# Twelve layers on one core: norms in halves, weight loads moved into the layers, one reordered load queue and one merged last layer

## Chip, cores and metric

The kernel runs on one core of one Trainium2 chip. The metric is the device time of one execution in microseconds (us), given as the median of several runs. All arithmetic is in float32.

## The reference, cut to what matters

A stream x of 8 batches x 64 tokens x 256 features goes through four blocks of three layers, each of the form x + f(layernorm(x)): L0_xattn, L0_attn, L0_ffn, L1_xattn and so on to L3_ffn.

```python
def _layernorm(x, axis=-1, eps=1e-05):
    m = jnp.mean(x, axis=axis, keepdims=True)
    v = jnp.var(x, axis=axis, keepdims=True)
    return (x - m) / jnp.sqrt(v + eps)
...
    x = x + _L0_xattn_ref(ctx_1024, _layernorm(x, axis=-1), mask_BxS2_bf1, ...)
    x = x + _L0_attn_ref(_layernorm(x, axis=-1), ...)
...
    x = x + _L2_xattn_ref(_layernorm(x, axis=-1), ctx_1024, ctx_1024, mask_BxSxS2_ff0, L2_xattn_Wq, L2_xattn_Wk, L2_xattn_Wv)
...
    x = x + _L3_ffn_ref(_layernorm(x, axis=-1), L3_ffn_W_qkv, L3_ffn_b_qkv, L3_ffn_W_gate, L3_ffn_b_gate, L3_ffn_W_experts, L3_ffn_b_experts)
```

The four xattn layers read a context of 8 x 1601 rows of 256 numbers. L0_xattn is a perceiver attention with 16 heads, whose keys are the normed context and the latents. L1_xattn is attention of 16 heads with one mask for all batches. L2_xattn is one head over the context, with a mask of its own for each batch (softmax of q times context plus mask, times context). L3_xattn is linear attention. The attn layers are self attention (L0, L3) and mamba scans (L1 both ways, L2). The ffn layers are mixtures of experts, and the last one, L3_ffn, is self attention and a mixture side by side, both of the same normed input:

```python
        attn = jnp.einsum('bqhd,bkhd->bhqk', q, k) / jnp.sqrt(jnp.asarray(hd, x.dtype))
        attn = jax.nn.softmax(attn, axis=-1)
        attn_out = jnp.einsum('bhqk,bkhd->bqhd', attn, v).reshape(B, S, D)
        gate = jax.nn.softmax(x @ W_gate + b_gate, axis=-1)
        top_g, top_i = jax.lax.top_k(gate, TOP_K)
        combine = jnp.sum(jax.nn.one_hot(top_i, E, dtype=x.dtype) * top_g[..., None], axis=2)
        expert_out = jnp.einsum('bsd,edf->bsef', x, W_experts) + b_experts
        moe_out = jnp.einsum('bsef,bse->bsf', expert_out, combine)
        return attn_out + moe_out
```

## The kernel before, in words

`program` (L3930) lays out one block of instructions per layer after another. Inside a block each engine has its own hand-written program and the engines meet at semaphores only; at the end of a block all engines meet, and `end_layer` (L519) clears the layer's semaphores. x lies as `x_tok`, NT = 4 tiles of P = 128 tokens x 256 features. Two buffers, `weights_a` and `weights_b`, hold a layer's weights and the next layer's: before each layer but the last, a block of its own (L3950 to L3953) has SP issue the load of the next layer's weights (`load_weights`, L3941).

Nearly every layer begins alike. VectorE (DVE) in `norm_vector` (L173) takes bn_stats of the four tiles (L178), bn_aggr (L181), adds epsilon (L183); ScalarE (ACT) in `norm_scalar` (L192) makes the reciprocal root by Ln and Exp (L196, L198); DVE then writes the normed `z_tok` tile by tile (L187) and signals once. TensorE (PE) meanwhile multiplies the identity with constants (`keep_busy`, L201, matmul at L204, 512 columns each, two calls, or four for the mamba), then `turn_tensor` (L207, L218) turns the eight 128x128 squares of z into PSUM; `zT` (in the trace `z_feat`) is copied from there, feature half 0 by ACT and half 1 by DVE, and the first projection waits for both.

**L0_xattn** (L770). Ahead of the main loop DVE norms the latents twice and scales them (L974, L975), norms the first batch's context tile group by group (`ctx_stats` L950, `ctx_norm` L965, scaled by GpSimd (POOL) at L1126 and L1128), and only then takes part in the loop over eight query pairs p (PE L1262 and L1270, ACT, DVE L1005). ACT has `ctx_rstd` (L1156) ahead of its loop as well.

**L1_xattn** (L1452). SP loads the first batch's context (L1545), the mask (L1549), and the other seven; two buffers. The next layer's weights were issued ahead of these, by the block before.

**L2_xattn** (L540). Four pairs u of batches. For each batch the context is loaded twice, with features on partitions (`ctx_feat`, L602, a ring of 3 buffers) and with tokens on partitions (`ctx_tok`, L532 and L533, a ring of 3), and for each pair two mask halves (`mask`, L607). SP issues in one order and stands at each wait: a feature buffer is free when the scores of its batch are done, a token buffer when its `mix` is done. PE runs `scores(0)`, and then for each u `scores(u+1)`, `turn_weights(u)`, `mix(u)` and `turn_mixed(u)`:

```python
                        if b >= RING:
                            sp.wait_ge(scored, (b - RING) // 2 + 1)
                        sp.dma_start(cT[b % RING][:, :, :], L.aps["ctx_feat"][b].rearrange("(k p) n -> p k n", p=P)
...
                        if b >= RING:
                            sp.wait_ge(mixed, (b - RING) // 2 + 1)
                        load_ctx_tok(sp, ck[b % RING], L.aps["ctx_tok"][b], ck_loaded[b % RING])
```

**L3_ffn** (L3807) calls `self_attention` (L222), a block, and then `experts` (L2623), another. The attention goes over four tiles: PE projects V (L440), q and k (L447), makes scores (L457), turns the weights (L465), weighs V (L476) and turns the result back (L486); DVE copies scores (L325), subtracts the maximum (L329, L330), divides (L336 to L338) and adds to x (L345, L352); `keep_busy` fills waits of PE at four places. `experts` begins with the gate (PE L2843, DVE L2588 to L2620, PE L2861), then has for each of 8 experts PE's eight matmuls (L2899) into one PSUM tensor and DVE's four scaled additions into x (L2772), one after the other, and ends with a bias matmul (L2911) and an addition (L2787).

## Time and profile before

| | |
|---|---|
| median of 3 runs | 3185.78 us (3185.38 to 3188.05) |
| profiled execution | 3181.54 us, its span 3179.8 us |
| mean granted TensorE clock | 0.947 of full speed |
| PE busy | 2795.1 us (88%) |
| DVE, ACT, POOL busy | 1643.3, 1091.3, 522.6 us (52%, 34%, 16%) |
| DMA | 271.40 MB, mean 85 GB/s |

The layers begin at these times of the profiled execution (us from the span's start), read off SP's first issue or the first norm instruction of each:

| | xattn | attn | ffn |
|---|---|---|---|
| L0 | 8 | 1253 | 1308 |
| L1 | 1353 | 1857 | 2152 |
| L2 | 2375 | 2512 | 2608 |
| L3 | 2774 | 3008 | 3062 |

In the profile L12 is line 12 of the kernel; PE is the matmul part of TensorE, PEld its weight loads, SPq the queue of SyncE's DMA issues. A bracket behind an instruction says how long its engine stood idle before it and what released it. "PEclk" is the granted clock as a share of full speed. Layer prefixes are left out of names: `L_ffn_expert_w` belongs to whichever ffn layer is running at that time.

### The profile page before, as it was taken

The numbers are of one execution on the slowest core, as the hardware profiler recorded it, in microseconds if no ns is written. First come the engines' busy times: TensorE is split into PE (matmuls) and PEld (weight loads), VectorE is DVE, ScalarE is ACT, GpSimd is POOL, SyncE is SP. The second block draws the span as 40 slices with busy tenths as digits, with TensorE's granted clock in tenths as the row PEclk, the third lists the DMA queues.
The fourth block names the chain that finished last, engine by engine and source line by source line (L and its number), as shares of the span: only waits on it lengthen the run. The fifth ranks groups of instructions, "written<-read, shape, count | busy, mean of one in ns | idle before, by whom it ended". The sixth has DMA issues, their size and how long they took to land. (4 is left out here: it accounts for less than half of the span.)

```text
span 3179.8 us, 43613 instructions
## 1 busy us (share of the span) xinstructions
PE 2795.1 (88%) x17456; PEld 1893.7 (60%) x17456; DVE 1643.3 (52%) x3618; ACT 1091.3 (34%) x1933; POOL 522.6 (16%) x280
## 2 busy tenths in 40 slices
PE   5899999999999998779999978998975689799876
PEld 2466666666666666545656535665962357688644
DVE  5556465655656443545555545763541250177563
ACT  2333333333333332225555436641321252211120
POOL 2112020202112000000000004761010041144200
PEclk8899999999999999889999989998987799899898
DMA  4123223131323211130100000115857338543001
GB/s 141 46 54 67 64 59 78 44 78 45 67 55 67 55 45 34 69 125 22 43 22 22 1 6 34 43 32 187 304 193 250 107 88 301 207 166 124 33 1 33
DMA packets 92096, 271.40 MB, mean 85 GB/s; under 512 B 7920, under 2 KB 57096, under 8 KB 85240
## 3 DMA queue, kind: packets, MB, share of 16 engines
q1 hardware_dynamic: 87896, 259.65, 26.9%
q0 software_dynamic: 2976, 8.13, 0.7%
q8 instruction: 138, 2.26, 0.3%
q10 hardware_dynamic: 1024, 0.86, 0.1%
q14 instruction: 62, 0.51, 0.1%
HBM read 256.64 MB, written 11.44 MB: 84 GB/s over the span
## 5 line engine op out<-in xcount | busy, mean ns | idle before, releaser
L1375 PE MATMUL L_xattn_bank<-L_xattn_keys_tok,L_xattn_probsT 119*128 119x257 f32 (+1 forms) x1792 | 451.5, 392 | 9.2 <-ACT L_xattn_probsT L1211 0.4
L1312 PE MATMUL L_xattn_wide<-L_xattn_keys_feat,weights_a 128*128 128x512 f32 (+2 forms) x1024 | 382.9, 517 | 1.3 <-DVE L_xattn_k_rnorm L1024 0.7
L1375 PEld LDWEIGHTS L_xattn_bank<-L_xattn_keys_tok,L_xattn_probsT 119*128 119x128 f32 (+1 forms) x1792 | 320.0, 190 | 96.1 <-issue 33.1
L1312 PEld LDWEIGHTS L_xattn_wide<-L_xattn_keys_feat,weights_a 128*128 128x128 f32 x1024 | 190.4, 191 | 151.8 <-issue 125.4
L1020 DVE COPY L_xattn_k_normed<-L_xattn_wide 128x833 f32<-128x833 f32 (+1 forms) x128 | 131.3, 1026 | 227.6 <-PE L_xattn_wide L1312 227.6
L2313 DVE TENSOR_TENSOR_SCAN L_attn_state<-L_attn_decay,L_attn_banks 128x1024 f32<-128x1024 f32 x80 | 182.7, 2286 | 69.6 <-PE L_attn_banks L2516 61.6
L1590 DVE CUSTOM_DVE_ANT_0 L_xattn_scores<-L_xattn_banks,L_xattn_mask 128x512 f32<-128x512 f32 (+1 forms) x256 | 131.5, 570 | 151.8 <-issue 151.8
L1126 POOL TENSOR_TENSOR L_xattn_keys_tok<-L_xattn_keys_tok,weights_a 119x1792 f32<-119x1792 f32 (+2 forms) x24 | 61.1, 2547 | 850.3 <-DVE L_xattn_keys_tok L965 850.3
L2419 POOL TENSOR_TENSOR L_attn_state<-L_attn_state,L_attn_C_rows 128x1024 f32<-128x1024 f32 x80 | 188.8, 2362 | 70.1 <-DVE L_attn_state L2313 70.1
L1205 ACT ACTIVATE L_xattn_scores<-L_xattn_scores,L_xattn_neg_max 128x833 f32<-128x833 f32 x128 | 119.6, 982 | 205.9 <-DVE L_xattn_neg_max L1045 205.9
L2516 PEld LDWEIGHTS L_attn_banks<-L_attn_B_diagonal,L_attn_dt_u_tok 128*128 128x128 f32 x1280 | 150.4, 193 | 66.3 <-issue 64.7
L1040 DVE CUSTOM_DVE_ANT_0 L_xattn_scores<-L_xattn_wide,L_xattn_mask_row 128x833 f32<-128x833 f32 x128 | 126.4, 1022 | 108.7 <-issue 108.7
L1656 ACT ACTIVATE L_xattn_probsT<-L_xattn_banks 128x512 f32<-128x512 f32 (+1 forms) x208 | 122.7, 597 | 163.6 <-PE L_xattn_banks L1728 163.6
L1211 ACT ACTIVATE L_xattn_probsT<-L_xattn_bank 119x512 f32<-119x512 f32 x128 | 76.4, 597 | 276.5 <-PE L_xattn_bank L1352 276.5
L3405 PE MATMUL L_ffn_banks<-L_ffn_slot_features,L_ffn_expert_w 128*128 128x128 f32 x1440 | 167.8, 277 | 3.0 <-DVE x_tok L3235 3.0
L2516 PE MATMUL L_attn_banks<-L_attn_B_diagonal,L_attn_dt_u_tok 128*128 128x128 f32 x1280 | 165.2, 283 | 3.9 <-ACT L_attn_B_diagonal L2375 3.9
L3405 PEld LDWEIGHTS L_ffn_banks<-L_ffn_slot_features,L_ffn_expert_w 128*128 128x128 f32 x1440 | 165.0, 193 | 3.8 <-DVE x_tok L3235 3.7
L1030 DVE TENSOR_TENSOR L_xattn_k_normed<-L_xattn_k_scale,L_xattn_k_normed 128x834 f32<-128x834 f32 x128 | 155.7, 1258 | 2.5 <-DMA L_xattn_k_scale<-L_xattn_k_scale_rows 2.5
L1728 PE MATMUL L_xattn_banks<-const,L_xattn_scores 128*128 128x128 f32 (+1 forms) x832 | 134.2, 288 | 24.7 <-DVE L_xattn_V L1581 10.7
L2406 POOL TENSOR_TENSOR L_attn_D_diagonal<-const,weights_a 128x256 f32<-128x256 f32 x2 | 1.2, 613 | 821.6 <-POOLq L3952 821.6
L1728 PEld LDWEIGHTS L_xattn_banks<-const,L_xattn_scores 128*128 128x128 f32 (+1 forms) x832 | 88.8, 142 | 79.3 <-issue 45.8
L1664 ACT ACTIVATE L_xattn_scores<-L_xattn_scores,L_xattn_neg_max 128x1601 f32<-128x1601 f32 x64 | 103.5, 1618 | 92.8 <-DVE L_xattn_neg_max L1593 92.8
(503 smaller groups left out, 4648.1 us busy)
## 6 DMA issues: line engine op xcount, KB each, us to landing
L_xattn_k_scale<-L_xattn_k_scale_rows SPq DMA_DIRECT2D x128, 417.0 KB, 5.0
L_xattn_ctx_feat<-in_ctx_feat SPq DMA_DIRECT2D x24, 1601.0 KB, 10.7
L_ffn_expert_w<-in_x_L_ffn SPq DMA_DIRECT2D x16, 2056.0 KB, 7.9
L_ffn_expert_w<-in_x_L_ffn SPq DMA_DIRECT2D x15, 1028.0 KB, 6.2
L_ffn_expert_w<-in_x_L_ffn SPq DMA_DIRECT2D x15, 1024.0 KB, 5.9
L_attn_C_rows<-L_attn_c_rows SPq DMA_DIRECT2D x48, 256.0 KB, 3.2
L_xattn_ctx_tok<-in_ctx_tok SPq DMA_DIRECT2D x8, 1536.0 KB
L_xattn_ctx_tok_and_one<-in_ctx_tok SPq DMA_DIRECT2D x8, 1536.0 KB
```

The source lines that it names most:

```text
L1020: nc.vector.tensor_copy(kn[:, s % 2, a:a + n], ps).then_inc(k_copied, 1)
L1030: nc.vector.tensor_tensor(k, spread[:, 2 * x:2 * x + 2, :], k, ALU.mult).then_inc(kn_ready, 1)
L1040: nc.vector.tensor_tensor_reduce(sc2[:, h, 0:HALF], ps, mrow[b % 2][:, :], 1.0, -3.0e38, ALU.add, ALU.max, mx[:, h:h + 1]).then_inc(s_take ...
L1312: last = nc.tensor.matmul(wide[:, 2 * h + c, 0:n], wk[:, k, p * P:(p + 1) * P], xnT[b % 2][:, k, a:a + n], start=(k == 0), stop=(k == KT - 1))
L1375: last = nc.tensor.matmul(bS[:, 0:D + 1], pT[0:r, c, a, :, :].rearrange("p h q -> p (h q)"), xn[b % 2][0:r, t, :], start=(i == 0), stop=(i ...
L1590: nc.vector.tensor_tensor_reduce(sc[:, j, a:a + n], ps[:, j, 0:n], mk[:, a:a + n], 1.0, -3.0e38, ALU.add, ALU.max, mx[:, j, c:c + 1]).then ...
L1656: nc.scalar.activation(pT[0:r, i % RING, :, :], ps[0:r, 6 + n % 2, :].rearrange("p (a n) -> p a n", n=P), ACT.Copy).then_inc(pT_ready, 1)
L1728: last = nc.tensor.transpose(ps[0:r, 6 + n % 2, j * P:(j + 1) * P], sc[:, j, t * P:t * P + r], L.ident)
L2313: nc.vector.tensor_tensor_scan(h[:, p % RING, :, :].rearrange("p m n -> p (m n)"), dA[:, p % RING, :, :].rearrange("p m n -> p (m n)"), ba ...
L2419: nc.gpsimd.tensor_tensor(state, state, C[:, g % C_RING, :].unsqueeze(1) .broadcast_to([P, 2, N]), ALU.mult).then_inc(hC_ready, 1)
L2516: last = nc.tensor.matmul(banks[:, i + j, t * P:(t + 1) * P], duT[d][:, t, m * P:(m + 1) * P], diag[:, g % DIAG_RING, t, :], start=True, s ...
L3405: last = nc.tensor.matmul(bank[:, c, :], w1[:, k, f:f + P], xT[:, j % 2, k, :], start=(k == 0), stop=(k == KT - 1))
```

## The change

It has five parts.

**Norms in halves.** `norm_vector` and `norm_scalar` work on tiles 0 and 1, then on 2 and 3, with a signal each; the addition of epsilon is gone (it is the bias of ACT's Ln). `turn_tensor` turns a token half as soon as it is ready; ACT copies token half 0 of `zT`, DVE half 1. `keep_busy` at these places is one matmul of 512 columns and one of 128 (the mamba keeps four for L1, one for L2).

```diff
+    for h in range(2):
+        for t in (2 * h, 2 * h + 1):
+            last = nc.vector.bn_stats(L.stats[:, t, :], x[:, t, :])
+        chain(last)
+        for t in (2 * h, 2 * h + 1):
+            last = nc.vector.bn_aggr(L.mv[:, t, :], L.stats[:, t, :])
+        last.then_inc(ln_stats_ready, 1)
...
+        nc.scalar.activation(rstd, L.mv[:, 2 * h:2 * h + 2, 1], ACT.Ln, bias=L.eps[:, 0:1]).then_inc(rstd_ready, 1)
...
-                keep_busy(L, ps[:, 7, :], 2)
-                pe.wait_ge(z_ready, 1)
-                turn_tensor(L, ps).then_inc(zT_turned, 1)
+                keep_busy(L, ps[:, 7, :], 1)
+                keep_busy(L, ps[:, 7, :], 1, 128)
+                turn_tensor(L, pe, ps, zT_turned, z_ready)
```

**Weight loads inside the layers.** The eleven blocks of their own are gone; each layer's SP program calls `L.load_next_weights(sp)`: first of all in the self attentions, mambas and ffn layers, behind the latents in L0_xattn, behind the first batch's context in L1_xattn and L3_xattn, behind all loads in L2_xattn.

```diff
-            if n + 1 < len(packs):
-                with nc.Block() as block:
-                    @block.sync
-                    def _(sp):
-                        load_weights(sp, n + 1)
```

On SP in L1_xattn, before (the context is `L1_xattn_ctx_feat`, `weights_a` the next layer's weights):

```order
L3941 DMA weights_a<-in_w_L1_attn 128x8116
L3952 UNCONDITIONAL_BRANCH
L1540 UNCONDITIONAL_BRANCH
L1545 DMA L1_xattn_ctx_feat_0<-in_ctx_feat 128x2x1601
L1549 DMA L1_xattn_mask<-in_mask_SS2 64x1601 x2
```

and after:

```order
L1947 UNCONDITIONAL_BRANCH
L1952 DMA L1_xattn_ctx_feat_0<-in_ctx_feat 128x2x1601
L1956 DMA L1_xattn_mask<-in_mask_SS2 64x1601 x2
L4058 DMA weights_a<-in_w_L1_attn 128x8116
L1952 DMA L1_xattn_ctx_feat_1<-in_ctx_feat 128x2x1601
```

The weights' load has moved from ahead of the first context batch to behind the mask.

**L0_xattn's first context batch inside the query loop.**

```diff
+                    if p in (1, 2):
+                        ctx_stats(0, p - 1)
+                    if p in (3, 4):
+                        ctx_norm(0, p - 3)
...
+                    if p in (2, 3):
+                        ctx_rstd(0, p - 2)
```

**L2_xattn's loads and steps.** The feature ring has FEAT = 4 buffers, the token ring stays at 3. The loads are issued in the order that the rows below show. PE and DVE go pair by pair:

```diff
-                scores(0)
                 for u in range(PAIRS):
-                    if u + 1 < PAIRS:
-                        scores(u + 1)
+                    scores(u)
+                    keep_busy(L, ps[:, 4, :], 4)
                     turn_weights(u)
                     mix(u)
                     turn_mixed(u)
```

On SP in L2_xattn, from the third feature load on, before (batch 2 into buffer 2, batch 3 into buffer 0, and so on):

```order
L602 DMA L2_xattn_ctx_feat_2<-in_ctx_feat 128x2x1601
L602 DMA L2_xattn_ctx_feat_0<-in_ctx_feat 128x2x1601
L607 DMA L2_xattn_mask_1<-in_mask_BSS2 64x1601 x2
L532 DMA L2_xattn_ctx_tok_2<-in_ctx_tok 128x12x256
L533 DMA L2_xattn_ctx_tok_2<-in_ctx_tok 65x256
L532 DMA L2_xattn_ctx_tok_0<-in_ctx_tok 128x12x256
L533 DMA L2_xattn_ctx_tok_0<-in_ctx_tok 65x256
L602 DMA L2_xattn_ctx_feat_1<-in_ctx_feat 128x2x1601
L602 DMA L2_xattn_ctx_feat_2<-in_ctx_feat 128x2x1601
```

and after:

```order
L988 DMA L2_xattn_ctx_feat_2<-in_ctx_feat 128x2x1601
L988 DMA L2_xattn_ctx_feat_3<-in_ctx_feat 128x2x1601
L1000 DMA L2_xattn_mask_1<-in_mask_BSS2 64x1601 x2
L919 DMA L2_xattn_ctx_tok_2<-in_ctx_tok 128x12x256
L920 DMA L2_xattn_ctx_tok_2<-in_ctx_tok 65x256
L988 DMA L2_xattn_ctx_feat_0<-in_ctx_feat 128x2x1601
L919 DMA L2_xattn_ctx_tok_0<-in_ctx_tok 128x12x256
L920 DMA L2_xattn_ctx_tok_0<-in_ctx_tok 65x256
L988 DMA L2_xattn_ctx_feat_1<-in_ctx_feat 128x2x1601
```

Batch 3's features have a buffer that nothing has used, and batch 4's features are issued ahead of batch 3's tokens.

**L3_ffn as one block.** `attention_and_experts` replaces both. The gate stands ahead of q and k, the experts' matmuls between the steps of the attention; ACT scales an expert's output by its gate weight (four 128x256 instructions each), POOL adds the eight outputs up in `experts_total`, and DVE adds that once to x at the end:

```diff
+                scale_expert(0)
+                exponentials(0)
+                exponentials(1)
+                scale_expert(1)
+                scale_expert(2)
+                copy_turned(0)
...
+                        nc.gpsimd.tensor_tensor(total[:, :, :], total[:, :, :], ys[e % 2][:, :, :], ALU.add).then_inc(y_added, 1)
...
+                dve.wait_ge(y_added, E)
+                chain(nc.vector.tensor_tensor(L.x[:, :, :], L.x[:, :, :], total[:, :, :], ALU.add))
```

On PE in L3_ffn from the scores on, before (L204 is `keep_busy`, L465 turns weights, L476 weighs V):

```order
L457 MATMUL L_ffn_banks<-L_ffn_kT,L_ffn_q_of_head 128x64 x64
L204 MATMUL L_ffn_banks<-const 128x512 x5
L465 MATMUL L_ffn_banks<-const,L_ffn_scores 128x128 x8
L204 MATMUL L_ffn_banks<-const 128x512 x2
L465 MATMUL L_ffn_banks<-const,L_ffn_scores 128x128 x8
L476 MATMUL L_ffn_banks<-L_ffn_probsT,L_ffn_V 32x2x64 x16
L204 MATMUL L_ffn_banks<-const 128x512
L476 MATMUL L_ffn_banks<-L_ffn_probsT,L_ffn_V 32x2x64 x16
```

and after (L832 is an expert's output, L842 turns weights, L853 weighs V):

```order
L821 MATMUL L_ffn_banks<-L_ffn_kT,L_ffn_q_of_head 128x64 x32
L832 MATMUL L_ffn_banks<-L_ffn_expert_w,z_feat 128x256 x8
L821 MATMUL L_ffn_banks<-L_ffn_kT,L_ffn_q_of_head 128x64 x32
L832 MATMUL L_ffn_banks<-L_ffn_expert_w,z_feat 128x256 x16
L842 MATMUL L_ffn_banks<-const,L_ffn_scores 128x128 x8
L832 MATMUL L_ffn_banks<-L_ffn_expert_w,z_feat 128x256 x8
L842 MATMUL L_ffn_banks<-const,L_ffn_scores 128x128 x8
L853 MATMUL L_ffn_banks<-L_ffn_probsT,L_ffn_V 32x2x64 x16
```

Where `keep_busy` stood, an expert's matmuls stand now; the other expert matmuls lie between the later steps.

## Rows read from the trace of the kernel before

**Rows 1.** Window in L0_xattn: us, busy PE PEld DVE ACT POOL, PEclk, DMA share, GB/s
```profile
120.00:400.00 280.00, 272.58 (x1514) 178.62 (x1512) 162.89 (x367) 103.83 (x157) 45.95 (x16) 1.00 0.27 61
```
**Rows 2.** Timeline at the start of L0_ffn: start us, us, engine, ...
```profile
1308.38 1.41 DVE L178 BATCH_NORM_STATS2 ln_stats<-x_tok 128x6 f32<-128x256 f32 x4 [1.78 <-PEq L3952]
```
**Rows 3.** Timeline at the start of L3_ffn, which has no such block
```profile
3062.39 0.75 DVE L178 BATCH_NORM_STATS2 ln_stats<-x_tok 128x6 f32<-128x256 f32 x2 [1.33 <-PEq L522]
```
**Rows 4.** Lines by form in the first 8 us of L0_attn (busy us, mean ns; idle before)
```profile
L178 DVE BATCH_NORM_STATS2 ln_stats<-x_tok 128x6 f32<-128x256 f32 x4 | 1.4, 413 | 2.0 <-PEq L3952 2.0
L187 DVE TENSOR_SCALAR z_tok<-x_tok,ln_mean_var,ln_rstd 128x256 f32<-128x256 f32 x4 | 1.4, 410 | 0.5 <-ACT ln_rstd L198 0.5
```
**Rows 5.** Windows at the start of L1_xattn and while it waits
```profile
1354.00:1358.00 4.00, 3.65 (x4) 1.10 (x4) 3.26 (x14) 1.69 (x3) 0.00 (x0) 0.57 1.09 365
1368.00:1377.00 9.00, 3.66 (x5) 1.60 (x6) 0.50 (x1) 0.00 (x0) 0.00 (x0) 0.50 1.02 287
```
**Rows 6.** Timeline of L0_xattn ahead of its main loop
```profile
30.58 2.39 DVE L950 BATCH_NORM_STATS2 L_xattn_ctx_stats<-L_xattn_keys_tok 119x6 f32<-119x256 f32 x7 [6.69 <-DMA L_xattn_keys_tok<-in_ctx_tok]
36.78 11.67 DVE L965 TENSOR_SCALAR L_xattn_keys_tok<-L_xattn_keys_tok,L_xattn_ctx_mean_var,L_xattn_ctx_rstd 119x256 f32<-119x256 f32 x14
37.90 2.07 PE L1270 MATMUL L_xattn_bank<-L_xattn_k_square,const 128*128 128x512 f32 x2 [7.32 <-ACT L_xattn_k_square L1172]
39.31 3.85 POOL L1126 TENSOR_TENSOR L_xattn_keys_tok<-L_xattn_keys_tok,weights_a 119x1792 f32<-119x1792 f32 x1 [38.85 <-DVE L_xattn_keys_tok L965]
```
**Rows 7.** Source line L965: all instructions, ns min/median/max
```profile
L965 DVE TENSOR_SCALAR L_xattn_keys_tok<-L_xattn_keys_tok,L_xattn_ctx_mean_var,L_xattn_ctx_rstd x112: 399/407/3940, 36.8 to 1020.3; 119x256 f32<-119x256 f32 x104, 54x256 f32<-54x256 f32 x8
```
**Rows 8.** Timeline of L1_xattn: issues, projections, first scores
```profile
1353.38 0.34 SPq L3941 DMA_DIRECT2D weights_a<-in_w_L_attn  x1
1354.11 0.37 SPq L1545 DMA_DIRECT2D L_xattn_ctx_feat<-in_ctx_feat  x1
1360.10 3.67 PE L1681 MATMUL L_xattn_banks<-z_feat,weights_b 128*128 128x512 f32 x8 [0.88 <-DVE z_feat L1561]
1373.34 13.77 PE L1695 MATMUL L_xattn_banks<-L_xattn_ctx_feat,weights_b 128*128 128x512 f32 x32 [9.57 <-DMA L_xattn_ctx_feat<-in_ctx_feat]
```
**Rows 9.** Timeline of L2_xattn: scores, exponentials, mixes, one SP issue
```profile
2391.46 5.60 PE L714 MATMUL L_xattn_banks<-L_xattn_ctx_feat,L_xattn_q_by_Wk 128*64 128x512 f32 x32 [0.69 <-ACT L_xattn_q_by_Wk L667]
2399.55 1.63 ACT L671 ACTIVATE L_xattn_scores<-L_xattn_scores,L_xattn_neg_max 128x1601 f32<-128x1601 f32 x1 [8.14 <-DVE L_xattn_neg_max L633]
2410.97 7.98 PE L714 MATMUL L_xattn_banks<-L_xattn_ctx_feat,L_xattn_q_by_Wk 128*64 128x512 f32 x32 [13.90 <-DMA L_xattn_ctx_feat<-in_ctx_feat]
2420.97 5.83 PE L741 MATMUL L_xattn_banks<-L_xattn_ctx_tok,L_xattn_probsT 128*64 128x256 f32 x52
2427.93 1.02 SPq L602 DMA_DIRECT2D L_xattn_ctx_feat<-in_ctx_feat  x2
2442.24 7.71 PE L714 MATMUL L_xattn_banks<-L_xattn_ctx_feat,L_xattn_q_by_Wk 128*64 128x512 f32 x32 [14.34 <-issue]
2496.55 8.08 PE L741 MATMUL L_xattn_banks<-L_xattn_ctx_tok,L_xattn_probsT 128*64 128x256 f32 x52 [4.37 <-DMA L_xattn_ctx_tok<-in_ctx_tok]
```
**Rows 10.** Windows of L2_xattn
```profile
2380.00:2400.00 20.00, 14.85 (x56) 6.48 (x56) 2.96 (x11) 3.43 (x6) 0.00 (x0) 0.96 1.05 344
2440.00:2460.00 20.00, 15.75 (x99) 7.99 (x99) 3.34 (x13) 3.46 (x6) 0.00 (x0) 0.84 0.54 156
```
**Rows 11.** Windows of L3_ffn: attention, experts; of L204 alone in the attention
```profile
3062.40:3116.40 54.00, 37.40 (x356) 23.13 (x356) 35.21 (x57) 15.28 (x23) 0.00 (x0) 0.90 0.00 1
3117.60:3175.30 57.70, 38.69 (x156) 30.62 (x156) 19.87 (x67) 0.23 (x1) 0.00 (x0) 0.87 0.13 36
...
3062.40:3116.40 54.00, 10.15 (x20) 3.83 (x20) 0.90 0.00 1
```
**Rows 12.** Source lines of like operations elsewhere: POOL's 128x1024 addition, ACT's 128x256 copy
```profile
L1984 POOL TENSOR_TENSOR L_xattn_k_tok<-L_xattn_k_tok,L_xattn_group_max x32: 619/1933/1937, 2791.8 to 2980.6; 128x1024 f32<-128x1024 f32 x24, 65x256 f32<-65x256 f32 x8
L3283 ACT ACTIVATE L_ffn_slot_out<-L_ffn_banks x30: 365/384/385, 2231.1 to 2756.6; 128x256 f32<-128x256 f32 x30
```

More of the change, by code:

```diff
@@ L176, in norm_vector @@
     x, z = x or L.x, z or L.z
-    for t in range(NT):
-        last = nc.vector.bn_stats(L.stats[:, t, :], x[:, t, :])
-    chain(last)
-    for t in range(NT):
-        last = nc.vector.bn_aggr(L.mv[:, t, :], L.stats[:, t, :])
-    chain(last)
-    nc.vector.tensor_scalar(L.rstd[:, :], L.mv[:, :, 1], EPS, None, ALU.add).then_inc(ln_stats_ready, 1)
-    dve.wait_ge(rstd_ready, 2 * (nx + 1))
-    for t in range(NT):
-        last = nc.vector.tensor_scalar(z[:, t, :], x[:, t, :], L.mv[:, t, 0:1], L.rstd[:, t:t + 1],
-                                       ALU.subtract, ALU.mult)
```

832 lines of the change are left out of this document (463 added, 369 removed).

## The prediction

> **What bounds the kernel now.** I first read the busy shares: PE is busy 88% of the span, so a stage where PE is full can't gain. The windows show where it is full: in L0_xattn's main loop PE is busy 272.6 of 280 us at clock 1.00 [rows 1]. That layer is 1245 us of the 3180, and the change touches only its first 60 us. So the gain must come from the stages where PE waits, and for these I read the timelines, stage by stage, asking what ends each wait. There are four kinds. At every layer's start everything waits for the block's end and for the norm [rows 2 to 4]. In L1_xattn PE stands 9.57 us for the first context batch [rows 8]. In L2_xattn PE stands 14 us in each pair [rows 9]. In L3_ffn PE is busy in 37.4 of 54 us and then in 38.7 of 57.7 [rows 11].
>
> **The sum, part by part.** All terms are against the profiled execution, 3181.54 us, which lies 4.2 us under the median of 3185.78; I apply the same saving to the median.
>
> *Block boundaries.* With a block of its own for the load DVE stands 1.78 us until its first bn_stats [rows 2]; where only the layer's own block ends, 1.33 [rows 3]. The difference is 0.45, and I take 0.5; the bounds are 0.3 and 0.8. Seven layers count here (L0_attn, L0_ffn, L1_attn, L2_attn, L2_ffn, L3_xattn, L3_attn): L1_xattn and L2_xattn have their own terms below, and L1_ffn waits for expert weights at its start. **3.5 us, bounds 2 to 6.** The issue of the weights now stands in the layer's own SP program ahead of the expert loads, as it stood before, so no transfer gets later there.
>
> *Norms in halves.* Per layer the first z half is ready earlier by half of bn_stats, and turning half 0 overlaps the second half of z: each of these steps takes 1.4 us for four tiles [rows 4], so at most 0.7 each, and the epsilon step (0.17) is gone. New are two more ACT instructions and semaphore hops in the chain. Against that, keep_busy is shorter. In L1_xattn's first 4 us the clock is 0.57 with four recorded matmuls in it [rows 5]; if PE does less there, turning and the first projection could run at the half clock for longer. I take 0.6 us per layer in the same seven layers: **4 us, bounds -3 to 9**, the lower if 0.4 us is lost in each by the clock.
>
> *L0_xattn before its loop.* DVE waits 6.69 us for the context, then does statistics and norms until 36.78 + 11.67 = 48.4, while PE has done its first projections and stands [rows 6]. After the change the query steps run beside it. But the norm instructions (L965) took 11.67 us for 14 where the median one takes 0.407 and the longest 3.94 [rows 6, 7], and they did so while POOL's multiplications of 3.85 us ran: DVE stood still for POOL. This will catch DVE inside the query loop now, and POOL's four multiplications, which the keys need, begin later than at 39.31. I take **3.5 us, bounds 0 to 8**: the loop's work (eight steps) gains up to 8 by starting early, and POOL's later start can take all of it. The Trainium skill (SBUF — State Buffer, section "SBUF: two separate sides") says that a DVE instruction with two SBUF inputs and a GpSimd instruction that reads SBUF exclude each other for a whole instruction. The stretched L965 agrees.
>
> *L1_xattn.* The next layer's weights (4058 KB) are issued at 1353.38, ahead of the first context batch (1601 KB) at 1354.11, and PE has its batch at 1373.34 [rows 8]. The channel moved 365 GB/s, later 287 [rows 5], so the weights alone hold it for 11 to 14 us. Behind the batch and the mask they hold up batch 1 instead, which has time, because a batch's projections take PE 13.8 us at a clock that was 0.50 in this wait and would be full. The next bound is the query projection, which ends at 1360.10 + 3.67 = 1363.8, and less the boundary and the norm about 1362.5. So PE begins about 10.8 us earlier, and some 1 to 3 us come from the clock. **12 us, bounds 8 to 16.**
>
> *L2_xattn.* Scores of consecutive pairs are 31.3 us apart (2410.97, 2442.24) [rows 9]. A pair loads 4 x 1601 + 2 x 400 = 7204 KB; at 344 GB/s = 336 KB/us, the rate of a full window [rows 10], that is 21.4 us. In the window 2440 to 2460 the share is 0.54 [rows 10]: the channel idles because SP stands at a token load's wait for the mix, with the next features queued behind it (issued at 2427.93, right after the mix that ended at 2426.8) [rows 9]. With four feature buffers and features ahead of tokens this goes. The serial chain of a pair is then: scores 5.6, until the exponentials are there 4.1 (2397.06 to 2401.18), turning and mixing 7.9 (2418.95 to 2426.80), result 1.1, in all 18.7 us, under 21.4: DMA bounds it. All loads are 4 x 7204 KB = 85.8 us from 2375.3, plus 2 to land: 2463. The last mix follows within about 8 to 11 us, 2471 to 2474, where it ended at 2504.6. Saving 31 to 33; at 287 GB/s (280 KB/us, [rows 5]) the loads end at 2480 and the saving is 14. The waits for buffers are the risk: token loads still have three buffers. keep_busy's four matmuls lie in the 4.1 us of waiting. **30 us, bounds 20 to 34.**
>
> *L3_ffn.* Before, 54 + 57.7 us with 1.3 between: 113. After, PE has 37.4 - 10.15 (keep_busy) + 38.7 = 66 us of work [rows 11]; some of it gets shorter because the clock stays up. DVE would have 35.2 + 19.9 = 55 even with all that it does in the experts' block, and it loses the scaled additions. ACT has 15.3 + 32 x 0.384 = 27.6, POOL 8 x 1.93 = 15.5 [rows 11, 12]. So PE bounds it: 66 plus about 4 for the norm at the start and 3 at the tail, where the last steps (weigh, copy, project, add) are serial. That is 73, a saving of **40 us, bounds 32 to 47** (the lower if a third of DVE's or ACT's work gets into PE's way).
>
> POOL's eight additions read and write SBUF just while DVE's subtractions and divisions have two SBUF inputs. By the rule of the section named above they would exclude each other, at worst 15.5 us more on DVE; by it the saving would be nearer 30. DVE has at least 18 us to spare in 73 by the numbers above, so only the tail's share counts, and I keep 40.
>
> Sum: 3.5 + 4 + 3.5 + 12 + 30 + 40 = **93 us**, so 3088.5 for a profiled execution and 3092.8 on the median's basis.
>
> **The rivals.**
> - *L2_xattn stays tied to its waits.* If the token loads' waits still hold the features, or a lower DMA rate comes with it, L2 gains 12 instead of 30: 3111. For it: three token buffers. Against: batch 4's features go out ahead of batch 3's tokens, shown in the order of loads. Chance 0.12.
> - *POOL and ACT hold L3 up.* Each expert needs a PSUM slot that ACT must scale first, and ACT stands in the order of its own program. If PE waits for that, L3 saves 25: 3108. Chance 0.14.
> - *The half clock at the layers' starts.* The clock was 0.57 with four matmuls [rows 5]; with fewer, each of ten layers could run its first projections slower by 3 us: 3093 + 30 = 3123. Chance 0.06.
> - *Slower than before.* Only L0_xattn's main loop is long enough. If its changed start leaves PE at 1.2 GHz for part of it, every us of PE work takes one more; more than 93 us of PE work at that level decides for slower, 8% of the loop. 150 us would give 3243. Against it: clock 1.00 over these 280 us of the loop [rows 1]. Chance 0.02.
> - *More than the sum.* Waits vanish, so the clock rises (mean 0.947), and L3 and L2 reach their upper bounds, L0 its 8 us: 3093 - 20 = 3073. Chance 0.10.
>
> **How the numbers follow.** The forecast, 3093, has the chance 0.56, with its own range 3081 to 3104. The range 3072 to 3116 takes in the first two rivals and the last. Every case but one is far beyond 0.2% (6.4 us, about what a measurement of this kernel can tell from no change): faster 0.97, within 0.2% 0.01, slower 0.02.
>
> **What would show it.** L1_xattn: first context projection at about 9 us after the layer's start, not 20. L2_xattn: scores about 21 us apart and DMA share near 1 in every window until the last load; wrong if PE's waits still end 31 us apart. L3_ffn: 73 us from norm to output, PE's waits under 10 us in sum; wrong if ACT's or POOL's step ends them. Boundaries: DVE idle 1.3 us ahead of each bn_stats. L0_xattn's main loop begins about 3 us earlier and has the same length. The forecast is wrong if L0's loop changes its length, or if clock 0.5 shows in the first projections of many layers.

## The result, and the profile after

The changed kernel takes 3092.09 us (median of 4 runs, 3085.62 to 3094.59) against 3186.91 us of the kernel before in the same comparison: a ratio of 0.9693, 95% interval 0.9668 to 0.9718. 95 us are gone where 93 were forecast. The profiled execution took 3085.62 us, its span 3083.6.

The page of the profile after: span, busy shares, granted clock.

```profile
span 3083.6 us, 43471 instructions
PE 2784.0 (90%) x17478; PEld 1896.7 (62%) x17478; DVE 1631.0 (53%) x3566; ACT 1111.8 (36%) x1993; POOL 539.7 (18%) x288
PEclk8899999999999999889999998999998988989989
```

PE's work is the same within 11 us (2795.1 before). What went is waiting. The table takes each layer from its first norm instruction to the next layer's, from the two profiled executions. The last column is the spread over the profiled executions of all kernels below that leave this layer's code as the change has it (one execution each); it says how well one reading can be trusted.

| layer | before | after | saved | other kernels, same code |
|---|---|---|---|---|
| L0_xattn | 1245.5 | 1241.2 | 4.3 | 1239.6 to 1245.2 |
| L0_attn | 54.4 | 55.8 | -1.4 | 54.3 to 55.9 |
| L0_ffn | 45.8 | 43.6 | 2.2 | 43.6 to 45.7 |
| L1_xattn | 504.6 | 492.6 | 12.0 | 491.0 to 492.4 |
| L1_attn | 294.4 | 291.6 | 2.8 | 290.7 to 291.6 |
| L1_ffn | 222.9 | 221.1 | 1.8 | 221.2 to 228.5 |
| L2_xattn | 137.1 | 108.5 | 28.6 | 111.4 to 113.3 |
| L2_attn | 95.2 | 92.6 | 2.6 | 92.1 to 93.8 |
| L2_ffn | 166.6 | 166.3 | 0.3 | 166.2 to 167.4 |
| L3_xattn | 234.3 | 231.1 | 3.1 | 231.1 to 231.8 |
| L3_attn | 53.2 | 55.7 | -2.5 | 55.7 |
| L3_ffn to the end | 117.4 | 75.8 | 41.6 | 75.8, once 78.1 |

The other 0.8 us lie ahead of the first layer. Two things stand out. The three large terms came out near the forecast. And both self attentions read slower. For L3_attn every kernel with this code says so; L0_attn took 54.3 to 54.5 us in five of the seven others, as before the change, and L0_ffn was longer in the same five.

Two readings flatter the change: 108.5 us is the shortest L2_xattn of all kernels with this code, and L1_ffn took 221.2 to 228.5 us elsewhere, so that its 1.8 us are no gain that can be shown.

**L1_xattn.** The timeline after, against [rows 8] (columns: start, us, engine, line, operation, tiles, idle before):

```profile
1353.22 6.72 PE L2089 MATMUL L_xattn_banks<-z_feat,weights_b 128*128 128x512 f32 x8 [0.87 <-DVE z_feat L1969]
1359.78 11.30 PE L2103 MATMUL L_xattn_banks<-L_xattn_ctx_feat,weights_b 128*128 128x512 f32 x32
```

The context projections begin 11.4 us after the layer's start (1348.34), 19.2 before, with no wait for a DMA. But the query projection ahead of them takes 6.72 us where it took 3.67 [rows 8]. No other execution of this layer's code showed that: in the eight other kernels with this start it took 3.67 us.

**L2_xattn.** Timeline and windows after, against [rows 9, 10]:

```profile
2369.70 5.60 PE L1121 MATMUL L_xattn_banks<-L_xattn_ctx_feat,L_xattn_q_by_Wk 128*64 128x512 f32 x32 [0.69 <-ACT L_xattn_q_by_Wk L1074]
2381.66 5.83 PE L1148 MATMUL L_xattn_banks<-L_xattn_ctx_tok,L_xattn_probsT 128*64 128x256 f32 x52
2388.62 5.60 PE L1121 MATMUL L_xattn_banks<-L_xattn_ctx_feat,L_xattn_q_by_Wk 128*64 128x512 f32 x32
2405.40 8.41 PE L1148 MATMUL L_xattn_banks<-L_xattn_ctx_tok,L_xattn_probsT 128*64 128x256 f32 x52 [4.78 <-DMA L_xattn_ctx_tok<-in_ctx_tok]
2414.83 5.60 PE L1121 MATMUL L_xattn_banks<-L_xattn_ctx_feat,L_xattn_q_by_Wk 128*64 128x512 f32 x32
```

```profile
2380.00:2400.00 20.00, 18.19 (x116) 9.73 (x114) 3.33 (x13) 4.41 (x8) 0.00 (x0) 1.00 1.04 345
2400.00:2420.00 20.00, 14.57 (x83) 7.61 (x84) 0.91 (x2) 1.00 (x3) 0.00 (x0) 0.83 1.06 328
2420.00:2440.00 20.00, 15.61 (x101) 8.88 (x99) 3.35 (x13) 3.56 (x6) 0.00 (x0) 1.00 1.05 314
2440.00:2450.00 10.00, 9.12 (x53) 4.73 (x51) 2.43 (x11) 3.57 (x6) 0.00 (x0) 1.00 0.64 210
```

Scores are 18.9 and 26.2 us apart, 31.3 before; the DMA share is 1.04 to 1.06 from 2380 to 2440, so the channel bounds the layer there. It is not so to the end: the last token load is issued at 2435.9, right after the third mix, and the share is 0.64 from 2440 to 2450:

```profile
2435.91 0.37 SPq L919 DMA_DIRECT2D L_xattn_ctx_tok<-in_ctx_tok  x1
```

That is 82.3 us after the layer's start; before, the last token load was issued 113.1 us after it (2489.18).

**L3_ffn.** The whole block as one window, and lines of DVE and PE in it (busy us, mean ns, idle us before), against [rows 11]:

```profile
3007.80:3081.50 73.70, 62.20 (x504) 47.25 (x504) 45.10 (x82) 28.10 (x58) 17.50 (x8) 0.92 0.09 31
```

```profile
L673 DVE TENSOR_TENSOR L_ffn_scores<-L_ffn_scores,L_ffn_sum 128x1024 f32<-128x1024 f32 x4 | 8.3, 2078 | 0.1
L665 DVE TENSOR_TENSOR L_ffn_scores<-L_ffn_scores,L_ffn_max 128x1024 f32<-128x1024 f32 x4 | 6.2, 1557 | 0.1
L664 DVE TENSOR_REDUCE L_ffn_max<-L_ffn_scores 128x16 f32<-128x1024 f32 x4 | 4.8, 1208 | 0.0
L842 PE MATMUL L_ffn_banks<-const,L_ffn_scores 128*128 128x128 f32 x32 | 4.2, 275 | 3.3 <-DVE L_ffn_scores L673 3.3
```

PE is busy 62.2 of 73.7 us. The last addition to x ends 71.2 us after the layer's start, and PE's waits within it add up to 6.4 us. DVE's steps end all of them (3.3 us are for the divisions), none is ended by ACT or POOL. The divisions (L673) take 2.08 us in the mean, the reductions 1.21 as ever.

**The starts.** The beginning of L3_attn, before and then after:

```profile
3009.22 3.75 PE L204 MATMUL L_attn_banks<-const 128*128 128x512 f32 x4 [5.01 <-PEq L3952]
3013.19 1.09 PE L218 MATMUL L_attn_banks<-const,z_tok 128*128 128x128 f32 x8 [0.22 <-DVE z_tok L187]
3015.16 3.69 PE L440 MATMUL L_attn_banks<-weights_a,z_feat 128*128 128x256 f32 x16 [0.88 <-DVE z_feat L299]
```

```profile
2952.17 1.32 PE L207 MATMUL L_attn_banks<-const 128*128 128x512 f32 x4 [3.85 <-PEq L909]
2954.81 1.97 PE L220 MATMUL L_attn_banks<-const,z_tok 128*128 128x128 f32 x8 [1.32 <-DVE z_tok L188]
2957.65 6.64 PE L451 MATMUL L_attn_banks<-weights_a,z_feat 128*128 128x256 f32 x16 [0.88 <-DVE z_feat L310]
```

The turn begins 2.64 us after the start instead of 3.97, but takes 1.97 us instead of 1.09, and the same 16 recorded matmuls take 6.64 us instead of 3.69. Windows over the second 7 us of the layer say why: the clock was 1.00 before and is 0.68 now, that is 1.2 GHz for part of the stretch and 2.4 for the rest. The first row is of before, the others of after (the first of these from the turn on: 0.50); the columns are those of [rows 1].

```profile
3016.20:3023.20 7.00, 7.00 (x24) 4.27 (x23) 0.00 (x0) 2.89 (x4) 0.00 (x0) 1.00 0.00 0
```

```profile
2955.20:2959.20 4.00, 3.12 (x12) 2.48 (x11) 1.21 (x4) 0.60 (x1) 0.00 (x0) 0.50 0.18 72
2959.20:2966.20 7.00, 7.00 (x19) 4.90 (x18) 0.00 (x0) 1.11 (x2) 0.00 (x0) 0.68 0.00 0
```

### The profile page after: what moved, and what is told of

It reads as the page before. It is cut to its first block and busy times, and to the rows that moved or that the text cites. A ratio compares the mean times of both kernels' runs of the same rounds, so it can differ in the third digit from the quotient of the medians.

```text
span 3083.6 us, 43471 instructions
## 1 busy us (share of the span) xinstructions
PE 2784.0 (90%) x17478; PEld 1896.7 (62%) x17478; DVE 1631.0 (53%) x3566; ACT 1111.8 (36%) x1993; POOL 539.7 (18%) x288
## 5 line engine op out<-in xcount | busy, mean ns | idle before, releaser
L2930 PEld LDWEIGHTS L_attn_banks<-L_attn_B_diagonal,L_attn_dt_u_tok 128*128 128x128 f32 x1280 | 150.9, 194 | 66.1 <-issue 64.5
L2136 PEld LDWEIGHTS L_xattn_banks<-const,L_xattn_scores 128*128 128x128 f32 (+1 forms) x832 | 88.4, 142 | 78.9 <-issue 45.8
```

The lines of the kernel that those rows point to most:

```text
L2136: last = nc.tensor.transpose(ps[0:r, 6 + n % 2, j * P:(j + 1) * P], sc[:, j, t * P:t * P + r], L.ident)
L2930: last = nc.tensor.matmul(banks[:, i + j, t * P:(t + 1) * P], duT[d][:, t, m * P:(m + 1) * P], diag[:, g % DIAG_RING, t, :], start=True, s ...
```

## Experiments

Each kernel is the changed one with the edit shown, unless said otherwise. Where a kernel has one execution, what is compared is the length of the layer in question in its profile, against the last column of the table.

### L1_xattn with the weights first

```diff
             def _(sp):
+                L.load_next_weights(sp)
                 for b in range(B):
...
-                        L.load_next_weights(sp)
```

> The changed kernel, with the next layer's weights issued ahead of the first context batch in L1_xattn again, and nothing else. If the order of these two loads made the 12.0 us that L1_xattn gained (504.6 to 492.6 us), PE waits some 9 to 10 us for the first batch again and L1_xattn takes 502 to 504 us. Rival: the gain came from the norm, the missing block and the clock; then L1_xattn stays within 2 us of 492.6.

L1_xattn took 501.4 us, against 492.6 after and 491.0 to 492.4 elsewhere; the whole 3103.26 us. PE waits as before, in its timeline:

```profile
1353.82 3.67 PE L2089 MATMUL L_xattn_banks<-z_feat,weights_b 128*128 128x512 f32 x8 [0.88 <-DVE z_feat L1969]
1366.83 5.36 PE L2103 MATMUL L_xattn_banks<-L_xattn_ctx_feat,weights_b 128*128 128x512 f32 x8 [9.34 <-DMA L_xattn_ctx_feat<-in_ctx_feat]
```

So the order of these two loads is worth 9 to 10 of the 12 us, and the rest came with the other parts. The query projection takes 3.67 us here with the same short keep_busy ahead of it that went with 6.72 in the changed kernel.

### L2_xattn with three places; with the old order of loads

```diff
-    FEAT = 4
+    FEAT = 3
```

> The changed kernel with three feature buffers instead of four in L2_xattn, the new order of loads kept. Theory A, the order matters and not the fourth place: the waits of the features for the scores are met before SP comes to them (it issued batch 5's features at 2395.6, scores of pair 1 ended at 2394.2), so L2_xattn stays at 108.5 to 111 us. Rival, the fourth place is needed: 115 us or more, PE waiting for features.

```diff
-                for u in range(1, PAIRS):
...
+                load_tok(3)
+                for u in range(2, PAIRS):
+                    load_feat(2 * u)
+                    load_feat(2 * u + 1)
+                    load_mask(u)
+                    load_tok(2 * u)
                     load_tok(2 * u + 1)
```

> The changed kernel with four feature buffers but the old order of loads in L2_xattn (features of both batches, masks, tokens of both, pair by pair), PE's new order kept. If the load order is what matters, the DMA share falls again in the middle of the layer and L2_xattn takes 118 us or more (up to 137 as before). Rival, PE's order (mix of a pair ahead of the next scores) is what matters: 109 to 114 us.

With three places L2_xattn took 113.3 us, with the old order of loads 109.3. The kernel with the weights first, in which L2_xattn is as the change has it, showed 113.3 as well, so both lie in the spread of the unchanged layer (108.5 to 113.3). The first lies between the two forecasts (up to 111, or 115 and more), the second is what the rival said. Neither of the two shows an effect by itself, as far as a spread of 5 us lets one see it. That contradicts the theory behind my forecast, and the next two tell where the gain is.

### L2_xattn with PE's old order; with only PE's new order

```diff
-                    scores(u)
-                    keep_busy(L, ps[:, 4, :], 4)
+                    if u + 1 < PAIRS:
+                        scores(u + 1)
                     turn_weights(u)
```

(`scores(0)` ahead of the loop, and DVE's `scores_taken(u + 1)` ahead of `divide(u)`. The four `keep_busy` matmuls of each pair are gone too; no run takes them out alone.)

> The changed kernel with PE's and DVE's old order in L2_xattn (scores of the next pair ahead of turning and mixing this one, no keep_busy), the new loads and four places kept. The unchanged L2_xattn took 108.5, 113.3 and 111.7 us in three kernels so far, and neither three places (113.3) nor the old order of loads (109.3) left that range. Theory now: what counts is that a pair's mix no longer waits behind the next pair's features, so token buffers come free earlier. Then L2_xattn takes 118 to 130 us here, with the channel idle in the middle. Rival: the gain needs all of it or came from elsewhere; then it stays within 108 to 114 us.

> The changed kernel with three places and the old order of loads in L2_xattn together; what remains of that part is PE's and DVE's order, keep_busy and the late weight load. Three places alone gave 113.3, the old load order alone 109.3, the old PE order 128.6, unchanged kernels 108.5 to 113.3. Theory A: the PE order carries the part by itself, so 109 to 115 us. Rival: either remedy on the load side is enough but one is needed; then 118 us or more.

With PE's old order L2_xattn took 128.6 us (the whole 3110.38). With PE's new order but three places and the old order of loads it took 110.8. The windows of the first, then of the second:

```profile
2380.00:2400.00 20.00, 8.01 (x24) 2.69 (x26) 1.22 (x7) 1.72 (x2) 0.00 (x0) 0.57 1.05 347
2400.00:2420.00 20.00, 8.56 (x77) 5.53 (x73) 3.34 (x13) 3.45 (x6) 0.00 (x0) 0.79 0.69 238
2420.00:2440.00 20.00, 15.72 (x99) 8.00 (x99) 3.34 (x13) 3.45 (x6) 0.00 (x0) 0.84 0.74 220
```

```profile
2382.00:2402.00 20.00, 14.81 (x84) 8.12 (x85) 2.00 (x10) 3.56 (x6) 0.00 (x0) 0.84 1.05 330
2402.00:2422.00 20.00, 15.42 (x101) 8.10 (x99) 3.34 (x13) 3.56 (x6) 0.00 (x0) 0.99 1.05 325
2422.00:2442.00 20.00, 18.48 (x105) 9.28 (x104) 2.61 (x12) 3.56 (x6) 0.00 (x0) 0.91 1.02 324
```

Before the last loads, the DMA share falls (to 0.69) only where PE does the next scores first. The timeline of that kernel shows the chain:

```profile
2391.99 8.53 PE L1121 MATMUL L_xattn_banks<-L_xattn_ctx_feat,L_xattn_q_by_Wk 128*64 128x512 f32 x32 [13.19 <-DMA L_xattn_ctx_feat<-in_ctx_feat]
2402.54 5.83 PE L1148 MATMUL L_xattn_banks<-L_xattn_ctx_tok,L_xattn_probsT 128*64 128x256 f32 x52
```

PE stands 13.19 us for pair 1's features while pair 0's weights are ready to be turned. Pair 0's mix ends at 2408.4, 49.4 us after the layer's start (2359.0), where it ended at 2387.5 after the change, 33.9 us after its start. The mix is what frees token buffers, so SP stands, and the channel runs dry. The last token load is issued 105.0 us after the layer's start (at 2464.06), 113.1 before the change and 82.3 after it. The load order and the fourth place are worth nothing that shows once the mix comes first. With the old PE order they and the later weight load and the start together gave 137.1 - 128.6 = 8.5 us. The new order (with its keep_busy) is worth 15 to 20 us beside the new loads (128.6 against 108.5 to 113.3).

### Two keep_busy matmuls again; norms whole again

```diff
-                keep_busy(L, ps[:, 7, :], 1)
-                keep_busy(L, ps[:, 7, :], 1, 128)
+                keep_busy(L, ps[:, 7, :], 2)
```

(The same at all starts with two; two instead of one in L2's mamba.)

> The changed kernel with two keep_busy matmuls of 512 columns at the layers' starts again, the norms in halves kept. Theory: the shorter keep_busy left PE at the 1.2 GHz level while it turned z and made the first projection (6.64 us instead of 3.69 in the self attentions), which ate the gain of the halves. Then the first projections take 3.7 us again, the self attentions take 53 to 54 us instead of 55.8, L1_xattn 490 instead of 492.6, in all 6 to 15 us less than the changed kernel. Rival: the halves themselves, by starting the turn earlier, are at fault; then nothing changes by more than 1 us in a layer, or each layer gets 1 us longer because PE is still in keep_busy when z is there.

On top of that, the norms whole:

```diff
+    for t in range(NT):
+        last = nc.vector.bn_stats(L.stats[:, t, :], x[:, t, :])
+    chain(last)
+    for t in range(NT):
+        last = nc.vector.bn_aggr(L.mv[:, t, :], L.stats[:, t, :])
+    last.then_inc(ln_stats_ready, 2)
+    dve.wait_ge(rstd_ready, 4 * nx + 4)
...
```

> The kernel with two keep_busy matmuls, and besides the norms whole again (statistics of four tiles, one reciprocal root, four tiles of z, then the turn); epsilon stays in ACT's Ln. If the halves are worth 0.6 us a layer, as forecast, the layers take 0.4 to 0.8 us more each than with halves and two keep_busy, 5 to 9 us in all (3092 to 3096). Rival: with PE in keep_busy until 3.8 us after the start the halves gain nothing, and it is equal within 2 us.

With halves and two keep_busy: 3087.37 us (3082.58 to 3089.56), ratio 0.9688, interval 0.9672 to 0.9704. The interval overlaps the changed kernel's, so the total doesn't prove the 5 us, and the 6 to 15 us expected did not come. In L3_attn the projection is fast again:

```profile
2955.24 2.75 PE L207 MATMUL L_attn_banks<-const 128*128 128x512 f32 x4 [3.85 <-PEq L907]
2957.88 1.95 PE L220 MATMUL L_attn_banks<-const,z_tok 128*128 128x128 f32 x8
2960.70 3.69 PE L450 MATMUL L_attn_banks<-weights_a,z_feat 128*128 128x256 f32 x16 [0.87 <-DVE z_feat L310]
```

The projection takes 3.69 us again, and L3_attn 52.7 us instead of 55.7; L2_ffn took 163.5 instead of 166.3. These two came out alike in the later kernels that have both the halves and this keep_busy (52.6 and 52.7, 163.1 and 163.4). L0_attn's projection stayed slow, at 5.35 us, and L1_xattn's was 3.67 in other kernels with the short keep_busy as well. L0_ffn and L3_ffn took 1.7 to 1.8 us more. Part of this is a shift between neighbours: L0_attn and L0_ffn were 55.8 and 43.6 in one execution of the same code and 54.4 and 45.7 in another, with sums of 99.4 and 100.1. By sums L0's pair gains 0.2 us and L3's 1.2.

With the norms whole: 3100.43 us (3097.40 to 3101.78), ratio 0.9733, interval 0.9714 to 0.9752, clear of the kernel with halves. The halves are worth 0.45% or 14 us by the ratios, 9.8 us by the two profiled spans, where 5 to 9 were expected. The largest part lies in L1_attn, whose norm runs twice (296.7 against 290.8 us). From the first bn_stats of L1_attn to the turn it is 7.2 us with halves (1842.31 to 1849.53), 9.2 whole (1844.63 to 1853.83). Not all of the 9.8 us is the shorter way to the turn, for the clock moved too: with the norms whole, L1_xattn's query projection took 6.16 us in spite of two keep_busy matmuls (3.67 with halves), and L2_ffn's first projection 3.36 instead of 1.99.

### One more keep_busy in the gap

On top of two, behind the turn at eight starts:

```diff
                 turn_tensor(L, pe, ps, zT_turned, z_ready)
+                keep_busy(L, ps[:, 7, :], 1, 256)
```

> The kernel with two keep_busy matmuls, and one more of 256 columns behind the turn at eight starts, where PE stands 0.8 to 0.9 us for the copies of zT. If the clock follows how busy PE was just before, the first projections that still ran slow with two (9.5 us in L1_attn where 7.0 is full, 6.5 in L3_ffn where 5.1 or less is full) get faster, 1 to 2 us a layer in some layers, 3 to 8 us in all. Rival: the matmul of 256 columns lengthens the gap where it runs at the low clock, or the clock doesn't notice; 0 to 3 us slower than with two.

3079.97 us (3079.00 to 3082.57), ratio 0.9669, interval 0.9649 to 0.9688. All four runs are below all four of the changed kernel. Against the kernel with two and no third (3087.37, interval 0.9672 to 0.9704) the intervals overlap, so what the third matmul adds is not shown by the totals. L2_attn took 90.4 us and L3_xattn 228.0 here, but the last kernel below, with the same code in both layers, took 93.0 and 231.2, as the kernel without the third did. What both kernels show is L3_ffn's V projection at full speed:

```profile
3008.11 1.05 PE L207 MATMUL L_ffn_banks<-const 128*128 128x256 f32 x2
3010.97 3.70 PE L803 MATMUL L_ffn_banks<-weights_b,z_feat 128*128 128x256 f32 x16
```

It took 5.39 us after the change and 5.08 before, and 6.51 with two keep_busy and no third; L3_ffn took 75.4 us, against 77.6 in that kernel and 75.8 after the change.

### The boundary alone

```diff
+                if n + 1 < len(packs):
+                    with nc.Block() as block:
+                        @block.sync
+                        def _(sp):
+                            load_next_weights(sp)
+                L.load_next_weights = lambda sp: None
```

(In the else branch of a test for the four xattn layers, which keep their load inside.)

> The changed kernel with the load of the next weights in a block of its own again ahead of the self attentions, mambas and ffn layers (seven layers that have a next one), the xattn layers unchanged. Forecast 0.5 us each: DVE stands 1.8 us instead of 1.33 ahead of the first bn_stats, and the time rises by 3.5 us. Rival: by up to 1.2 us each (in L3_attn it stood 2.49 us before), so 6 to 9 us.

3088.86 us (3085.60 to 3100.53), ratio 0.9705, interval 0.9677 to 0.9734: no difference that the total can tell. The waits ahead of the first bn_stats do tell it. L3_attn in the changed kernel, then in this one:

```profile
2952.17 0.75 DVE L180 BATCH_NORM_STATS2 ln_stats<-x_tok 128x6 f32<-128x256 f32 x2 [1.33 <-PEq L909]
```

```profile
2955.89 0.75 DVE L180 BATCH_NORM_STATS2 ln_stats<-x_tok 128x6 f32<-128x256 f32 x2 [2.07 <-PEq L4079]
```

The same in five other layers: 1.24 and 1.99, 1.05 and 1.78, 1.33 and 2.06, 1.18 and 1.91, 1.22 and 2.25. (The seventh, L1_attn, has no such wait ahead of its first bn_stats.) A block costs 0.73 to 0.75 us in five of the six, 1.03 in one. Six of them are 4.7 us. So the waits give the price of a block, and no total shows it as time. Both self attentions even came out shorter (53.3 and 52.4 us against 55.8 and 55.7), and L3_ffn, which has no such block and whose code is unchanged, longer (78.1 against 75.8). The clock is what differs. L3_attn here, to be read against its rows after the change:

```profile
2958.52 1.66 PE L220 MATMUL L_attn_banks<-const,z_tok 128*128 128x128 f32 x8 [0.59 <-DVE z_tok L188]
2961.06 3.69 PE L451 MATMUL L_attn_banks<-weights_a,z_feat 128*128 128x256 f32 x16 [0.88 <-DVE z_feat L310]
```

The keep_busy is the same short one, and the projection takes 3.69 us, not 6.64; L0_attn's does too. The keep_busy matmuls themselves took 2.05 us here and 1.32 after the change, and PE stood 0.59 us behind them instead of 1.32. So the length of keep_busy alone does not decide the clock of the next projection; where a layer starts and at which level count as well. No run moves the start alone.

### L0_xattn's context first; POOL's additions

```diff
+                for piece in range(2):
+                    ctx_stats(0, piece)
+                for piece in range(2):
+                    ctx_norm(0, piece)
                 for p in range(NQ):
...
```

(Their places inside the loop are gone, and ACT's `ctx_rstd` is ahead of its loop.)

> The changed kernel with the first context batch's statistics and norms ahead of the query loop again. L0_xattn took 1241.2 us after the change, 1245.5 before. If the interleaving made this, it takes 1244 to 1246 us. Rival, the norm or the later weight load made it: 1241 to 1242. Unchanged kernels gave 1239.6 to 1243.9 in L0_xattn, so the reading is the start of the first turning of keys (63.1 us after the change, 68.1 before), which should be 67 to 68 us by the first theory.

The first turning of keys began at 66.1 us (67 to 68 expected), against 63.1 after and 68.1 before, and L0_xattn took 1244.9. The interleaving is worth 3.0 us at that place; the other 2 us came with the other parts.

```diff
-                        nc.gpsimd.tensor_tensor(total[:, :, :], total[:, :, :], ys[e % 2][:, :, :], ALU.add).then_inc(y_added, 1)
+                        nc.gpsimd.tensor_tensor(total[:, 0, 0:8], total[:, 0, 0:8], ys[e % 2][:, 0, 0:8], ALU.add).then_inc(y_added, 1)
...
```

> The changed kernel, but POOL adds only 8 columns of each expert's output in L3_ffn, and the last output alone is added to x (the sum of the other seven is left out). In the changed kernel DVE's subtractions and divisions took 1.22 us alone and 3.22, 2.30 and 2.65 us where POOL's addition ran. Theory: they exclude each other, and these 4.5 us of DVE standing lie partly on the path, so that L3_ffn gets 2 to 5 us shorter (75.8 to 71 to 74 us) and every such DVE instruction takes 1.2 us. Rival: PE, busy 62 us of 74, bounds it; then DVE's instructions get short but L3_ffn stays within 1 us.

L3_ffn took 71.8 us instead of 75.8. The two DVE lines of this kernel:

```profile
L665 DVE TENSOR_TENSOR L_ffn_scores<-L_ffn_scores,L_ffn_max 128x1024 f32<-128x1024 f32 x4 | 4.9, 1225 | 0.1
L673 DVE TENSOR_TENSOR L_ffn_scores<-L_ffn_scores,L_ffn_sum 128x1024 f32<-128x1024 f32 x4 | 4.9, 1224 | 0.1
```

In the changed kernel they lost (2078 + 1557 - 1225 - 1224) x 4 = 4.7 us beside POOL, and the layer gets 3.9 us back, although PE is the busier engine: its wait for the divisions falls from 3.3 us to 0.2. This kernel also shortens POOL's own step; the kernel in the next section, in which POOL is busy longer and DVE less held up, tells the two apart.

### The gap filled, and POOL's additions in pieces

```diff
-                        nc.gpsimd.tensor_tensor(total[:, :, :], total[:, :, :], ys[e % 2][:, :, :], ALU.add).then_inc(y_added, 1)
+                        for t in range(NT):
+                            last = nc.gpsimd.tensor_tensor(total[:, t, :], total[:, t, :], ys[e % 2][:, t, :], ALU.add)
+                        last.then_inc(y_added, 1)
```

> The kernel with two keep_busy matmuls and the one in the gap, and in L3_ffn POOL's additions of 128x1024 cut into four of 128x256. If DVE and POOL exclude each other for a whole instruction, DVE now waits for a piece of 0.5 to 0.6 us instead of up to 2.0 us, its subtractions and divisions take 1.2 to 1.8 us, and L3_ffn gets 1.5 to 3.5 us shorter than the 75.3 us of the kernel without pieces (cutting POOL's work down to 8 columns gave 3.9). Rival: POOL gets the port again for each piece right away, so that DVE waits for all four; then L3_ffn is the same within 0.5 us. In all 3076 to 3079 us against 3080 for the kernel without pieces.

L3_ffn took 72.5 us, 75.4 without the pieces. DVE's and POOL's lines:

```profile
L722 POOL TENSOR_TENSOR L_ffn_experts_total<-L_ffn_experts_total,L_ffn_expert_out 128x256 f32<-128x256 f32 x28 | 23.4, 868 | 15.8 <-ACT L_ffn_expert_out L767 15.5
L673 DVE TENSOR_TENSOR L_ffn_scores<-L_ffn_scores,L_ffn_sum 128x1024 f32<-128x1024 f32 x4 | 6.1, 1515 | 0.1
L665 DVE TENSOR_TENSOR L_ffn_scores<-L_ffn_scores,L_ffn_max 128x1024 f32<-128x1024 f32 x4 | 5.2, 1288 | 0.1
```

DVE gets in between the pieces; now POOL is the one that waits, and it has the time: its 28 pieces are busy for 23.4 us, its eight steps were for 17.5, and still the layer is shorter. PE's wait for the divisions is 1.2 us here. In all 3078.28 us (5 runs, 3070.73 to 3087.65), ratio 0.9670, interval 0.9648 to 0.9693. The runs of this kernel spread wider than the 2.9 us in question, so the total can't tell it from the 3079.97 of the kernel without pieces. Both are below the changed kernel in the median, by 12 and 14 us; the intervals of the ratios still overlap its own (0.9668 to 0.9718).

## Why the prediction was right, point by point

- **The sum:** 93 us forecast, 95 measured (by the two medians of the comparison), 96 between the profiled executions. It is closer than its terms deserve. The block boundaries were priced too low and the norms too high, by about 2 us each; L3_ffn gave 1.6 more, L0_xattn 0.8 more and L2_xattn 1.4 less; and 2.6 us of the 96 lie where nothing was forecast, in L1_ffn and ahead of the first layer. That these cancel is luck.
- **Block boundaries:** mis-sized. I took the wait of one layer with such a block [rows 2] and that of another without [rows 3], 0.45 us apart. In the same layer the waits before and after are 0.72 to 0.78 us apart (L0_ffn: 1.78 and 1.05), and 1.16 in L3_attn. The error was to compare different layers, whose waits differ anyhow. Seven times 0.75 is 5.3, not 3.5. That is the price by the waits; the kernel that puts the seven blocks back was no slower in all.
- **Norms in halves:** the step that was wrong in kind as well as in size. I put the gain of the halves at 0.6 us a layer with the clock already in it. The halves with two keep_busy matmuls are worth more: the turn starts 1.3 us earlier (3.97 to 2.64 us after the start in L3_attn), and 9.8 to 14 us in all by the kernel with whole norms, a part of it the clock's. In the changed kernel the clock took much of that back. Its profile shows four first projections slower than before: by 3.0 us in L3_attn, 2.9 in L0_attn, 3.1 in L1_xattn and 1.9 in L2_xattn (5.56 instead of 3.67). Only two of them are steady. Over the eight kernels that start these layers as the change does, L3_attn's took 6.63 to 6.70 us and L0_attn's 5.12 to 6.73; counting the kernel with blocks too, L1_xattn's was slow in one execution of nine and L2_xattn's in three. My rival priced this at 3 us a layer in ten layers; it is real at that price in two, and I had called the forecast wrong if it showed in many. That the shorter keep_busy is the cause is only partly shown: two matmuls cured L3_attn, but not L0_attn (5.35; 3.69 only with the third matmul), and the short keep_busy with a block ahead of it gave 3.69 in both. The seven layers of these two terms together saved 7.1 us, 7.5 were forecast; less 5.3 for the boundaries, the norms brought about 2 where 4 were forecast.
- **L0_xattn:** 3.5 forecast, 3.0 shown by the kernel that undoes it, and 4.3 in the layer. DVE was indeed caught behind POOL inside the loop: its second set of seven norms took 8.26 us, the first 2.34. The first turning of keys began 5 us earlier, where I had the main loop 3 us earlier. The same layer's code spreads from 1239.6 to 1245.2, so only the start of the key turning resolves this term.
- **L1_xattn:** 12 forecast, 12.0 measured, 9 to 10 of them by the loads' order. I forecast a start of the context projections about 9 us after the layer's start; it was 11.4, because the query projection ran at the low clock for a part in this execution.
- **L2_xattn:** 30 forecast, 28.6 measured (23.8 to 28.6 by the spread of 108.5 to 113.3). The size was right because the serial chain of a pair, 18.7 us, is under the 21.4 us of its loads, and these I had worked out: scores came 18.9, 26.2 and 21.7 us apart. The channel moved 314 to 345 GB/s, not 344 all along, and the last token load still waited for a mix, so the last mix ended 100.7 us after the start and not at 96 to 99. My own case of 287 GB/s (14 us) lay outside my bounds of 20 to 34. The reason was half wrong. I had written that four places and features ahead of tokens make the wait go. It is the mix ahead of the next scores that does: 128.6 us without it, 110.8 with it and neither of the other two. My rival that the waits stay fell for the same reason; it argued from the token places, and these come free earlier by PE's order.
- **L3_ffn:** 40 forecast, 41.6 measured; 73 us from norm to output forecast, 71.2 to the last addition. PE's work was 62.2 us, 66 expected, and its waits were under 10 us, as I had put down. No run undoes the merge or the move of the scaled additions, so how the largest term divides among them is read from the profile alone. What I had left out of the sum on the grounds of DVE's slack was the exclusion of DVE and POOL, and it cost up to 3.9 us. POOL's additions also took 2.34 to 2.37 us each, not the 1.93 of [rows 12]. The Trainium skill (SBUF — State Buffer, section "SBUF: two separate sides") was right about the mechanism: instructions with two SBUF inputs wait, the reductions with one do not. L965 [rows 6, 7], which I took for agreement, is not such a case: it has one SBUF tensor and two values per partition, so that it stood as well is more than the rule as I quoted it says. 10 us, which I gave as its price, was too much. Slack in the sum of busy time was no argument, since PE waits for DVE's divisions in the middle of the layer (3.3 us).
- **The rival of a slower L0_xattn** fell: the layer got no longer (1239.6 to 1245.2 us, 1245.5 before).

## What to carry to other kernels

When one engine does the next round's first step ahead of this round's last, look at which buffers the last step frees: putting it first was worth 15 to 20 us here, while a fourth buffer and another order of loads showed nothing beside it. Filler matmuls at a stage's start are not idle time to be trimmed without a look at the next stage: with 384 columns fewer, L3_attn's first projection took 3 us more. But check such an effect in more than one execution and layer: the same filler left other projections alone, and one of the four slow ones never came back. To price a boundary or a wait, compare the same place in two kernels or two rounds, not two places.
